# A graph network kernel: edge terms laid in the ring by one DMA, key and value rows added to them by accumulating gathers, and no rests of GpSimd in the three edge stages

## What is computed

```python
h = relu(layernorm(x))
logit = tanh(h @ W1.T) @ w2                              # "pool"
x = x + segment_sum(softmax_by_dst(logit[src]) * h[src], dst)

h = relu(layernorm(x))
def conv(x, We, heads):                                  # twice: 8 heads of 16 ("multi"), 1 head of 128 ("single")
    q, k, v = x @ Wq + bq, x @ Wk + bk, x @ Wv + bv
    e = edge_attr @ We                                   # 200000 x 128, one row for each edge
    alpha = sum(q[dst] * (k[src] + e)) / sqrt(C)         # per head
    w = softmax_by_dst(alpha)
    return segment_sum((v[src] + e) * w, dst) + x @ Ws + bs
out = x + conv(relu(conv(h, We0, 8)), We1, 1)
```

## Time and profile before

| | |
|---|---|
| median of 3 executions | 8751.74 us |
| the profiled execution, its own time | 8750.25 us |
| its span in the profile | 8748.3 us |
| busy: PE, weight load, DVE, ACT, POOL | 72%, 52%, 60%, 32%, 52% |
| TensorE's granted clock, mean | 0.816 |
| pool gathers, first to last | 257 to 2485 us |
| multi gathers to the end of its items | 2884 to 5796 us |
| single gathers to the end of its items | 6086 to 8520 us |

### The profile page before, as it was taken

How to read it: one execution, slowest core, us unless ns; L and a number is a source line. 1 busy time by engine, 2 the same in 40 slices (tenths; PEclk the granted TensorE clock), 3 DMA queues, 4 the chain that set the end, 5 groups by cost and what they waited for, 6 DMA issues and landing times. The chain is left out here.

```text
span 8748.3 us, 177087 instructions
## 1 busy us (share of the span) xinstructions
PE 6293.5 (72%) x37309; PEld 4520.2 (52%) x37309; DVE 5246.4 (60%) x16838; ACT 2808.0 (32%) x6528; POOL 4508.2 (52%) x4707
## 2 busy tenths in 40 slices
PE   3455565566643678787787888865778888899998
PEld 2445555555531455555555555542455555555555
DVE  5344444455555888899998998863333444444452
ACT  2222233333310233333333333321333334444441
POOL 0566666666620566655554444411556666666550
PEclk6677777888876788888888888876888989999995
DMA  2333333333333444433333333334344444444442
GB/s 60 76 73 73 75 74 76 79 79 80 81 87 108 114 109 107 107 103 101 98 96 92 92 94 86 88 85 115 86 90 91 95 96 100 100 104 107 105 101 59
DMA packets 1195650, 796.51 MB, mean 91 GB/s; under 512 B 629426, under 2 KB 1086096, under 8 KB 1194616
## 3 DMA queue, kind: packets, MB, share of 16 engines
q0 software_dynamic: 175168, 411.90, 19.0%
q1 hardware_dynamic: 1019448, 373.53, 18.2%
HBM read 715.50 MB, written 69.42 MB: 90 GB/s over the span
## 5 line engine op out<-in xcount | busy, mean ns | idle before, releaser
L686 POOL DMA_INDIRECT ring_multi<-kv_rows,src_cols x1564 | 1549.9, 991 | 1722.0 <-DVE kv L794 492.0
L1085 POOL DMA_INDIRECT ring_single<-h_rows,src_cols x1564 | 1477.4, 945 | 1275.1 <-DMA ring_single<-h_rows,src_cols 470.7
L1085 POOL DMA_INDIRECT ring_pool<-pool_rows,src_cols x1564 | 1478.5, 945 | 1004.1 <-issue 421.3
L1198 PE MATMUL ps_s_pool<-ident,row_pool 128*128 128x128 f32 x1952 | 398.5, 341 | 875.8 <-issue 854.0
L1159 DVE CUSTOM_DVE_ANT_0 masked_pool<-mask_pool,ps_s_pool,start_pool 128x512 f32<-128x512 bf16 x488 | 364.6, 747 | 846.1 <-issue 787.4
L922 PE MATMUL ps_e_multi<-w_edge,attrT 64*128 64x512 f32 x976 | 591.3, 688 | 258.7 <-DVE kv L794 256.1
L1198 PEld LDWEIGHTS ps_s_pool<-ident,row_pool 128*128 128x128 f32 x1952 | 277.6, 173 | 962.4 <-issue 961.7
L1245 ACT ACTIVATE row_pool<-ring_pool 128x520 f32 x488 | 309.0, 633 | 1415.4 <-POOLq L1076 1415.4
L1213 PE MATMUL ps_p_pool<-row_pool,probT_pool 128*128 128x129 f32 x3904 | 714.5, 342 | 61.9 <-DVE probT_pool L1172 60.1
L905 PE MATMUL ps_p_multi<-message_multi,onehot 128*128 128x136 f32 x3904 | 729.7, 347 | 0.8 <-issue 0.8
L1213 PEld LDWEIGHTS ps_p_pool<-row_pool,probT_pool 128*128 128x128 f32 x3904 | 654.9, 253 | 104.0 <-issue 103.6
(11 more groups left out here) (219 smaller groups left out, 12509.3 us busy)
## 6 DMA issues: line engine op xcount, KB each, us to landing
dst_pool<-in_dst_rows SPq DMA_DIRECT2D x488, 128.0 KB
dst_single<-in_dst_rows SPq DMA_DIRECT2D x488, 128.0 KB
query_multi<-query_parts SPq DMA_DIRECT2D x488, 96.0 KB
cols<-query_cols SPq DMA_DIRECT2D x488, 64.0 KB
ring_pool<-pool_rows,src_cols POOLq DMA_INDIRECT x1564
ring_multi<-kv_rows,src_cols POOLq DMA_INDIRECT x1564
ring_single<-h_rows,src_cols POOLq DMA_INDIRECT x1564
edge_tail<-in_edge_cols SPq DMA_DIRECT2D x488, 34.0 KB
```

The costliest lines, as they stand in the source:

```text
L686: pool.indirect_dma_start(out=ring[:, u, j, :], out_offset=None, in_=rows, in_offset=bass.IndirectOffsetOnAxis(ap=g.src_cols[:, c:c + 1], ...
L1085: pool.indirect_dma_start(out=ring[:, u, j, :], out_offset=None, in_=rows, in_offset=bass.IndirectOffsetOnAxis(ap=g.src_cols[:, c:c + 1], ...
L1198: i = T_.transpose(ps_s[p1][:, j * P:(j + 1) * P], row[:, u1, j, D + 1:D + 2].to_broadcast([P, P]), g.ident[:])
```

## The change

1. **Pool stage, new work for each of the 391 blocks.** SP loads 16 attribute columns (`edge_in`, 16 x 512), TensorE multiplies them with `w_edge` (16 x 128) into `ps_e` (4 matmuls), ScalarE copies `ps_e` to `edge_out` (128 x 512), and SP stores that to a new DRAM table `edge_rows` (256 KB for a block). At the end of the stage SP waits for the stores.
2. **Multi stage.** `kv`, `attr`, `attrT`, `w_edge` and `ps_e` go, with the instructions at L725, L794, L886, L922 and L964. SP now only fills ring slots: for each block one DMA copies `edge_rows[n]` into the slot twice, into its key half and its value half (512 KB written in pieces of 512 bytes). It waits for `message` of the last item of block n - 8, the slot's last reader. GpSimd waits for that fill and then issues its four gathers with `compute_op=ALU.add`, so that key and value rows are added to what lies in the slot. The ring has 8 slots instead of 4. VectorE's `prod` and `message` read the ring; `prod` moves ahead, to where `kv` stood. The loads of `reset` and `query` are issued by ScalarE, 4 items ahead.
3. **Rests.** `landed_row(n, j - 1)` after the fourth gather goes in all three stages. `announce` stays.
4. `QB`, the number of query buffers in multi and single, goes from 4 to 8.

```diff
         @block.gpsimd
         def _(pool):
...
             for n in range(BLOCKS):
                 u = n % R
-                if n >= R:
-                    pool.wait_ge(ring_read.sem, items_done + ring_read.base)
-                    settle(g, pool)
+                pool.wait_ge(prefilled[u], attrs_base[u] + (n // R + 1) * 16)
                 for j in range(J):
                     c = n * J + j
                     pool.indirect_dma_start(
-                        out=ring[:, u, j, :], out_offset=None, in_=rows,
+                        out=ring[:, u, j].rearrange("p a c -> p (a c)"), out_offset=None, in_=rows,
                         in_offset=bass.IndirectOffsetOnAxis(ap=g.src_cols[:, c:c + 1], axis=0),
+                        compute_op=ALU.add,
                     ).then_inc(gathered[n % 2][j], 16)
                     if j == 1 and n >= 1:
                         announce(n - 1)
-                    if j == J - 1 and R <= n + 1 < BLOCKS:
-                        items_done = pool.value_load(g.block_ends[0:1, n + 1 - R:n + 2 - R], min_val=1, max_val=ITEMS)
-                    if j == J - 1:
-                        landed_row(n, j - 1)
             announce(BLOCKS - 1)

         @block.sync
         def _(sp):
+            for n in range(BLOCKS):
+                u = n % R
+                if n >= R:
+                    items_done = sp.value_load(g.block_ends[0:1, n - R:n - R + 1], min_val=1, max_val=ITEMS)
+                    sp.wait_ge(E["message"].sem, items_done + E["message"].base)
+                    settle(g, sp)
+                sp.dma_start(ring[:, u], g.edge_rows[n].unsqueeze(2).to_broadcast([P, J, 2, D]))\
+                  .then_inc(prefilled[u], 16)
...
# dense_stage
-                    if j == J - 1 and n % 2 == 1:
-                        landed_row(n, j - 1)
...
+            def edge_store(k):
+                B_["edge_sb"].wait(sp, k)
+                sp.dma_start(g.edge_rows[k], edge_out[:, k % EB]).then_inc(g.edge_stored[k % EB], 16)
...
+                if not single and has(n, BLOCKS):
+                    B_["edge"].wait(sp, n - U)
+                    sp.dma_start(edge_in[:, u], t["edge_cols"][0:EDGE_DIM, n * EDGES_B:(n + 1) * EDGES_B])\
+                      .then_inc(g.attrs_loaded[u], 16)
+                if not single and has(n - 6, BLOCKS):
+                    edge_store(n - 6)
...
+                if not single and has(n, BLOCKS):
+                    landed(pe, g.attrs_loaded, attrs_base, n, u)
+                    B_["edge_sb"].wait(pe, n - 2)
+                    for j in range(J):
+                        i = T_.matmul(ps_e[u % 2][:, j], edge_in[:, u, j * P:(j + 1) * P], w_edge[:],
+                                      start=True, stop=True)
+                    i.then_inc(B_["edge"].sem, 1)
...
+                k = n - 1
+                if not single and has(k, BLOCKS):
+                    B_["edge"].wait(act, k)
+                    if k >= EB:
+                        act.wait_ge(g.edge_stored[k % EB], k // EB * 16)
+                    S_.activation(edge_out[:, k % EB], ps_e[k % 2][:], ACT.Copy).then_inc(B_["edge_sb"].sem, 1)
```

More of the change, by code:

```diff
@@ L591, in blocks_gathered, with multi_stage @@
         g.gathered_base[k] += len(range(k, BLOCKS, 2)) * 16
-def edge_stage(g, kind, rows, width, heads, ring_blocks):
+def multi_stage(g, rows, ring_blocks):
     nc, t = g.nc, g.t
     V, S_, T_ = nc.vector, nc.scalar, nc.tensor
-    E, H, R = g.edge, heads, ring_blocks
-    pool_k, multi, single = kind == "pool", kind == "multi", kind == "single"
-    acc_w = {"pool": D + 1, "multi": H * HW, "single": ACC_W}[kind]
-    query_w = ACC_W if single else D
+    E, H, R = g.edge, HEADS, ring_blocks
+    acc_w = H * HW
@@ L758, in step @@
                     a5 = g.acc[:, ds(items.tile(u, 5), 1), 0:acc_w]
-                if multi and has(m5, ITEMS):
                     E["factor"].wait(dve, m5)
@@ L918, in step @@
                       .then_inc(E["prefix"].sem, 1)
-                if multi and has(n, ITEMS):
-                    E["attrT_sb"].wait(pe, n)
-                    E["kv"].wait(pe, n - 1)
-                    T_.matmul(ps_e[:], attrT[:, u % 2], w_edge[:].rearrange("k j c -> k (j c)"),
-                              start=True, stop=True).then_inc(E["edge"].sem, 1)
                 if has(m3, ITEMS):
@@ L978, in step @@
                       .then_inc(E["absent"].sem, 1)
-                if not multi and has(n, ITEMS):
-                    E["partial"].wait(act, n - U)
-                    act.wait_ge(blocks_ready, items.block(u) + (1 + blocks_base))
-                    settle(g, act)
-                    S_.activation(row[:, u, :, 0:copied], in_ring(items, u, 0, 0, copied), ACT.Copy)\
-                      .then_inc(E["rows"].sem, 1)
+                if has(n + AHEAD, ITEMS):
+                    fetch(n + AHEAD, u, AHEAD)
                 if has(m3, ITEMS):
@@ L1130, in _ @@
             rolled(sp, ITEMS, U, 0, step, items.begin, peel=ITEMS // U)
+            if not single:
+                for k in range(EB):
+                    sp.wait_ge(g.edge_stored[k], 16 * len(range(k, BLOCKS, EB)))
         @block.vector
```

296 lines of the change are left out of this document (116 added, 180 removed).

## The result

The changed kernel takes 8978.30 us (median of 4; 8957.61 to 8989.88) where the kernel before takes 8760.98 (4; 8746.28 to 8772.95): ratio 1.0246, 95% interval 1.0217 to 1.0275. It is 2.5% slower; the forecast was 8215, and its range ended at 8700. Spans: 8955.8 after, 8748.3 before.

A forecast was written before the change was run, and what follows sets the result against it. Gathering was taken to bound pool, gathering with TensorE close behind single, and VectorE multi. Gains of 90 (pool) + 150 (single) + 295 (multi) = 535 us against 8750 gave 8215 us, range 7880 to 8700.

The forecast's parts named there:

- pool, rests gone: Pool stage: without rests landing waits come back, between 27 and 142 us; the middle, -90 us, was taken.
- pool, new work: Pool stage: added matmuls (572 us TensorE) and copies (233 us ScalarE) hide under the gathers, costing nothing.
- single: Single stage: of 387 us of landing waits 225 remain without rests, 162 come back; taken as -150 us.
- multi: Multi stage: without `kv`, the larger of 6.5 us a block and VectorE's demand gives 2617 us, -295 us.
- Its issue: ... I take it as no dearer: Multi, GpSimd: issuing an accumulating gather costs the same 0.99 us as a plain one.
- 4.2 us: Multi: an accumulating gather lands 4.2 us after issue (plain 2.8), giving 1.6 us of idle a block.
- VectorE at 4.87 us an item: Multi: freed of `kv`, VectorE takes 4.87 us for each of 488 items, 2380 us.
- Some 110 waits of 1.0 us remain: Pool: with no rests some 110 announcement waits of 1.0 us remain, and 142 us come back.
- Rival A: Multi: additions are free, gathers cost and land as plain ones; total 7998, down to 7880; chance 0.15.
- Rival B: Multi, GpSimd: the addition doubles a gather's issue to 1.98 us, 9.1 us a block; total 9180; chance 0.12.
- Rival C: Multi: DMA engines become the limit, 7.1 us a block; total 8383, up to 8700 with slower additions; chance 0.15.
- Rival D: Pool and single: rests come back as announcement waits, nothing is won there; total 8455; chance 0.10.

## Why the prediction was wrong

By the terms of its sum:

| term | forecast | measured | where it went |
|---|---|---|---|
| pool, rests gone | -90 (142 less 52 for denser traffic) | -187 | without the edge work |
| pool, new work | 0 | +417 | 270 of it by the store's place in SP's queue |
| single | -150 | -254 | rests 178, QB some 40, the remainder open |
| multi | -295 | +252 | the gather's issue |

- **"Its issue: ... I take it as no dearer"** is the step that failed in multi. It measured 1.588 us, beyond the middle of the bounds 0.99 and 1.98 that I had set; I took the lower end because the plain gather was the only row. The middle, put into my own formula, would have said 4 x 1.49 + 0.9 + 0.6 of idle, some 7.5 us a block, 2930 us and no gain in this stage. The run without the addition shows it: the stage is then 2492 us, and nothing else was changed.
- **"4.2 us" for the landing and 1.6 us of idle**: too much. The fourth gather lands after 3.4 us with the addition and 2.9 without, so adding costs about half a microsecond, and the longer issue hides part: 0.77 us of idle. The 2.8 us that I halved and added was itself a misreading: it came from the 287 waits that were long enough to show, and over all blocks the gather that a rest waits for lands after 2.1 us. The fill, which my sum gave no part in the landing, adds 0.9 us.
- **VectorE at 4.87 us an item**: too much. It was not the limit in the changed kernel (2054 us busy of 3164), and where it nearly is, late in the run without the addition, an item takes 4.5 us.
- **New work in pool: "hidden"**. TensorE and ScalarE were, to within 3% of their sizes. What was not is the sentence "That SP waits for an edge store ... is hidden too". I asked whether the mask comes in time, and it does; I did not ask what the load, sent at another moment, lands on. With the store on ScalarE's queue, so that SP waits for no copy, 270 of the 417 us come back.
- **"Some 110 waits of 1.0 us remain"** was too dark: without the new work 56 remain, 60.6 us. The price for dense traffic, 1.41 us, came out: (558.4 - 323 x 0.305) / 323 = 1.42 us. That is in part luck, since with the same traffic and the store moved a wait costs (202.6 - 145 x 0.305) / 145 = 1.09 us. And 323 waits paid it, not 160.
- **Single**: mechanism right, under-sized, and "`QB` costs and brings nothing" was false by some 40 us. TensorE, at clock 0.96 in place of 0.91, left room down to 2067 us (late announcement in the kernel before).
- **Rival A** falls by the group row. **Rival B** had the right place, side and mechanism, and its deciding point held: it said that the stage loses what the others gain from 8.05 us a block on; the block took 8.04 and the stage lost 252, but pool and single together brought 24 us, not 240. Its price for the addition, 0.99 us a gather, was too much; 0.60 was measured. **Rival C** falls by the small fill. **Rival D** (rests come back as announcement waits) is false for the rests themselves, since they were pure loss with and without the edge work; in pool the announcement waits came with that work.
- The Trainium skill ("GPSIMD Engine Reference", When to use GPSIMD) has one core writing reads and one writes. Were the two lists written side by side, and an addition's second read the whole of the slower one, 1.98 us would follow; the trace has 1.588. A part of the 0.99 us that is fixed, as the prediction's own counter-argument said, would fit that; no run tests it. Another reading fits too: with the addition q0 has 128 packets a gather instead of 32, so the price may go by descriptors that are no longer joined, and not by a second read.
- The 46 ns that multi's gathers take beyond pool's were laid beside VectorE's density, with the rule of the Trainium skill ("SBUF — State Buffer", SBUF: two separate sides). The runs speak against that as the main cause: without rests a gather in multi takes 951 ns (1487.23 / 1564) with VectorE 90% busy, and 994 without the addition with VectorE 82% busy. What makes the 991 stays open.

The chance of "slower" was 0.13. The bounds were there, but the range took rival B out as a whole, though 0.60 of its 0.99 us was enough once pool and single did not bring their 240.

## What to carry to other kernels

An addition moved into a gather is not free for the engine that writes descriptors: it costs 0.6 times the gather again, so count it against GpSimd before taking work off VectorE, and if only the bounds are known, ask at what price the sign turns. Wait for a landing as late as the consumer allows (one gather later brought 749 us in this kernel, 261 in the kernel before), and add no rests to let transfers catch up. When a step puts one more wait into a queue's program, look at what is behind it in the queue: a load sent in step with every announcement can fall on the same gather most times.

## What the runs showed of the hardware

- An accumulating gather of 128 rows takes GpSimd 1.55 us with 512-byte rows and 1.59 with 1024, a plain one 0.945 and 0.95 to 0.99. In multi q0 then has one packet of 1024 bytes a row, 128 a gather, where plain ones have 32 of 4096 (325312 packets for the 175168 of before, the same bytes).
- What a gather's landing pays for, in multi, fourth gather: 2.0 us plain, 0.4 more for the addition with a small fill, 0.9 more for the fill's traffic alone, 1.4 more for both.
- The moment of other transfers counts: with the same ones in pool, the fourth gather landed after 3.1 us with the store in SP's queue, whose transfers then went in step with it, and 2.3 with the store in ScalarE's. The Trainium skill ("DMA: Bandwidth & Descriptors", Queues, rings and completion order) has each DMA engine take turns between its queues packet by packet. A gather beside a load should then be late by some of the load's packets, and the trace agrees in kind: 3.3 us beside the 128 KB load, 2.7 otherwise. The turns themselves no run here shows.
- TensorE's granted clock was higher where gathers came sooner: the same instructions in pool took 1921 us at 0.73 in the changed kernel (2458 us long), 1739 at 0.81 with the store moved (2188), and 1630 at 0.85 with the late announcement (2038).
- The kernel before took 24 and 27% longer in two series (10875 and 11123 against 8765 us), and an edit changed its sign there. The gathers' own times were the same.
